# A pre-norm transformer block: four score steps between the last feed-forward products, and a group's evacuation on VectorE

## What is computed

```python
x = x + 0.5 * ffn(layernorm(x))       # 8 experts, each 128 -> 256 -> 128
x = x + attn(layernorm(x))
x = x + 0.5 * ffn(layernorm(x))

# ffn: every token goes through all experts; g = top-1 gate
h = gelu(einsum('nd,edh->neh', xf, w1) + b1)
y = einsum('neh,ehd->ned', h, w2) + b2
out = (y * (g / (g + 1e-6))[:, None, None]).sum(axis=1)

# attn: second layernorm, then
q, k, v = split(xn @ w_qkv);  q, k = l2norm(q), l2norm(k)
o = softmax(causal(8.0 * q @ k.T)) @ v;   return o @ w_out
```

## Time and profile before

| | |
|---|---|
| median of 3 runs | 308.84 us (308.37 to 308.96) |
| the profiled execution | 308.51 us, its span 306.8 us |
| PE busy | 283.4 us (92%) |
| ACT busy | 226.5 us (74%) |
| DVE busy | 218.2 us (71%) |
| POOL busy | 86.4 us (28%) |

### The profile page before, as it was taken

The page is one execution under the profiler, slowest core; times in us unless marked ns, Lnnn a source line. Parts: engine busy times, 40 slices in busy tenths (PEclk is TensorE's granted clock), DMA queues, the critical chain, the costliest instruction groups (busy, mean ns, idle before and its releaser), DMA issues.

```text
span 306.8 us, 5263 instructions
## 1 busy us (share of the span) xinstructions
PE 283.4 (92%) x1699; PEld 198.4 (65%) x1699; DVE 218.2 (71%) x572; ACT 226.5 (74%) x347; POOL 86.4 (28%) x151
## 2 busy tenths in 40 slices
PE   7799999999949997689997989999999999999994
PEld 7588788688738885424432433248888878878882
DVE  5888888979867777695466362118778887888675
ACT  2477777776674776998797889986667787686672
POOL 7243103201860183190406604030230310320010
PEclk9699999999998999979999999999999999999999
DMA  5800000000000000000000000000000100100101
GB/s 166 241 24 3 0 1 2 0 1 0 2 1 0 0 4 0 0 2 0 2 2 1 3 0 2 0 2 0 0 2 1 35 2 0 34 0 0 35 2 34
DMA packets 8044, 4.66 MB, mean 15 GB/s; under 512 B 626, under 2 KB 8020, under 8 KB 8020
## 3 DMA queue, kind: packets, MB, share of 16 engines
q1 hardware_dynamic: 8020, 4.35, 4.9%
HBM read 3.30 MB, written 1.05 MB: 14 GB/s over the span
## 4 chain that ended last, share of the span: by engine, by line
PE 62%; DVE 12%; issue 11%; POOL 8%; ACT 6%; DVEq 0%; POOLq 0%; ACTq 0%
PE ps L412 8%; PE ps L422 8%; PE ps L414 7%; PE ps L413 7%; PE ps L553 7%; PE ps L424 7%; PE ps L423 7%; ACT probs L737 2%; PE ps L532 2%; DVE xn L833 2%; POOL rstd L1122 2%; DVE h_lo L887 2%; PE ps L400 2%; PE ps L590 1%; PE ps L584 1%
## 5 line engine op out<-in xcount | busy, mean ns | idle before, releaser
L724 ACT ACTIVATE h<-ps,cols 128x512 f32<-128x512 f32 x128 | 87.9, 689 | 51.3 <-PE ps L414 45.7
L887 DVE TENSOR_TENSOR h_lo<-h,h_hi 128x512 fp32r<-128x512 f32 x128 | 88.8, 697 | 30.7 <-ACT h_hi L727 27.8
L737 ACT ACTIVATE probs<-ps 128x1024 f32<-128x1024 f32 (+1 forms) x80 | 68.6, 964 | 7.5 <-PE ps L532 7.3
L422 PE MATMUL ps<-h_hi,w_hi 128*128 128x512 f32 x128 | 54.1, 422 | 4.2 <-DVE h_lo L887 3.4
L412 PE MATMUL ps<-xT_hi,w_hi 128*128 128x512 f32 (+1 forms) x128 | 51.9, 406 | 1.4 <-DVE xT_lo L1074 1.4
L414 PE MATMUL ps<-xT_hi,w_lo 128*128 128x512 f32 (+1 forms) x128 | 51.2, 400 | 0.0
L413 PE MATMUL ps<-xT_lo,w_hi 128*128 128x512 f32 (+1 forms) x128 | 51.0, 399 | 0.0
L424 PE MATMUL ps<-h_hi,w_lo 128*128 128x512 f32 x128 | 50.4, 394 | 0.0
L423 PE MATMUL ps<-h_lo,w_hi 128*128 128x512 f32 x128 | 50.4, 394 | 0.0
L727 ACT ACTIVATE h_hi<-ps,cols 128x512 fp32r<-128x512 f32 x72 | 49.1, 681 | 0.0
L1196 POOL TENSOR_SCALAR_AFFINE_SELECT probs<-probs 128x256 f32<-128x256 f32 x64 | 26.3, 434 | 55.2 <-ACT probs L737 54.4
(11 more groups left out here) (127 smaller groups left out, 299.9 us busy)
## 6 DMA issues: line engine op xcount, KB each, us to landing
w_raw<-in_L_ffn_w SPq DMA_DIRECT2D x8, 256.0 KB, 4.3
x_sb<-in_L_attn_x SPq DMA_DIRECT2D x4, 256.0 KB, 6.3
out_x<-x_sb SPq DMA_DIRECT2D x3, 256.0 KB, 2.3
out_x<-x_sb SPq DMA_DIRECT2D x2, 128.0 KB, 1.8
wqkv_sb<-in_L_attn_w_qkv SPq DMA_DIRECT2D x1, 96.0 KB, 4.9
wout_sb<-in_L_attn_w_out SPq DMA_DIRECT2D x1, 32.0 KB, 4.0
small<-in_L_ffn_b SPq DMA_DIRECT2D x1, 8.0 KB
small<-in_L_attn_ln_w SPq DMA_DIRECT2D x1, 0.5 KB
```

What stands on the lines that cost most here:

```text
L422: pe.matmul(y, w2_hi[:, w], h_hi[:, c % RING, :], start=(c == 0), stop=False)
L724: first = nc.scalar.activation(h[:, slot, :], ps[:, BANK_H + slot, :], ACT.Gelu, bias=bias)
L737: nc.scalar.activation(probs[:, s % P_SLOTS, :, 0:width], ps[:, bank:bank + 2, 0:width], ACT.Exp, scale=SCALE).then_inc(exp_done, 1)
L887: dve.tensor_tensor(h_lo[:, slot, :], h[:, slot, :], h_hi[:, slot, :].bitcast(f32), ALU.subtract).then_inc(split_done, 1)
```

## The change

Four things are done at the turn from the last feed-forward group of layer 0 to attention.

- The scores of steps 1, 2 and 3 move forward on PE: step 1 behind the qkv products at chunk 13, step 2 behind down(14), step 3 behind down(15). They, and step 0, use two sets of banks by turns (0 and 1, 2 and 3), so step 2 waits for the exp of step 0, and step 3 for that of step 1. From step 4 on three sets are used in turn again, beginning with banks 4 and 5; `score_set` and `set_reader` say which set and whose exp.
- The exp of step 1 moves in front of `evacuate_y` on ACT.
- The squares and copies of group 2 (six instructions) leave ACT. DVE makes the copies, then the squares from the copy in one instruction of 512 columns.
- In the last group the k copy of group 1 moves from ACT (chunk 12) to DVE (chunk 15).

```diff
--- before.py
+++ after.py
@@ -244,6 +244,14 @@
         jobs += [(quad_steps, "rows", u), (quad_steps, "features", u), (quad_steps, "project", u)]
         assert len({at for at, *_ in jobs}) == len(jobs) - 2
         job_number = {(kind, arg): n for n, (_, kind, arg) in enumerate(jobs)}
+
+        def score_set(s):
+
+            return s % 2 if s < 4 else (s - 2) % S_SETS
+
+        def set_reader(s):
+
+            return s - 2 if s in (2, 3) else None if s == 4 or s < 2 else s - S_SETS
 
         def output_bank(u):
             return 7 - u % 2
@@ -485,6 +493,10 @@
                         ln_transpose(ATT, g - 1, min(g + 2, GROUPS))
                     if operands and g >= 1 and c == at["att_qkv"]:
                         qkv_products(g - 1)
+                    if operands and last and c >= at["att_qkv"]:
+                        if c == at["att_qkv"]:
+                            pe.wait_ge(gelu_done, CHUNKS * GROUPS)
+                        scores(1 + c - at["att_qkv"])
 
             def qkv_products(p):
                 if p == 0:
@@ -521,15 +533,15 @@
 
             def scores(s):
                 st = steps[s]
-                if s >= S_SETS:
-                    pe.wait_ge(exp_done, s - S_SETS + 1)
+                if set_reader(s) is not None:
+                    pe.wait_ge(exp_done, set_reader(s) + 1)
                 for kt, q0, width, at in st["item"]:
                     k0 = SEQ * st["b"] + P * kt
                     qc = SEQ * st["b"] + GROUP * st["qg"] + q0
                     for hd in range(2):
                         j = 2 * st["pair"] + hd
                         rows = slice(ROW * j, ROW * j + ROW)
-                        m = pe.matmul(ps[:, 2 * (s % S_SETS) + hd, at:at + width], kT[rows, st["quad"], k0:k0 + P],
+                        m = pe.matmul(ps[:, 2 * score_set(s) + hd, at:at + width], kT[rows, st["quad"], k0:k0 + P],
                                       qT[rows, st["quad"], qc:qc + width], start=True, stop=True)
                 m.then_inc(scores_done, 1)
 
@@ -622,15 +634,12 @@
                         else:
                             pe.wait_ge(job_emptied, job_number["k_stack", p] + 1)
                     for s in (2 * k, 2 * k + 1):
-                        if s == 0:
+                        if s < 4:
                             continue
-                        if s < S_SETS:
-                            if s == 1:
-                                pe.wait_ge(gelu_done, CHUNKS * GROUPS)
-                            else:
-                                pe.wait_ge(qkv_copied, LAST)
-                                pe.wait_ge(y_evac, GROUPS)
-                                pe.wait_ge(xf_done[FFN], GROUPS)
+                        if s == 4:
+                            pe.wait_ge(qkv_copied, LAST)
+                            pe.wait_ge(y_evac, GROUPS)
+                            pe.wait_ge(xf_done[FFN], GROUPS)
                         scores(s)
                     if k == 0:
                         y_transposes(LAST, BANK_YT_LAST)
@@ -733,7 +742,7 @@
                 if s >= P_SLOTS:
                     act.wait_ge(pv_done, (s - P_SLOTS) // 2 + 1)
                 width = sum(w for _, _, w, _ in steps[s]["item"])
-                bank = 2 * (s % S_SETS)
+                bank = 2 * score_set(s)
                 nc.scalar.activation(probs[:, s % P_SLOTS, :, 0:width], ps[:, bank:bank + 2, 0:width], ACT.Exp,
                                      scale=SCALE).then_inc(exp_done, 1)
 
@@ -760,8 +769,7 @@
                         nc.scalar.activation(table_use[:, 1:2], ones[:, 0:1], ACT.Exp)
                     if operands and c == CHUNKS - 1 and last:
                         exp_scores(0)
-                        square_qk(g - 1)
-                        copy_qkv(g - 1)
+                        exp_scores(1)
                     if c == CHUNKS - 1:
                         evacuate_y(F)
                     if c + LAG < CHUNKS:
@@ -775,7 +783,7 @@
                             copy_qkv(g - 2)
                         if c == at["qk_high"]:
                             high_stacks(g - 2)
-                        if c == at["k_copy"]:
+                        if c == at["k_copy"] and not last:
                             copy_k(g - 2)
                     if operands and g >= 1 and c == at["att_copy"]:
                         affine_features(g - 1)
@@ -801,7 +809,7 @@
             for c in range(LAG):
                 gelu(0, 0, c)
             ffn_groups(nc.scalar, 0, lambda g: ffn_group(0, g))
-            for s in range(1, len(steps)):
+            for s in range(2, len(steps)):
                 exp_scores(s)
             for c in range(LAG):
                 gelu(1, GROUPS, c)
@@ -917,8 +925,27 @@
                 dve.tensor_scalar(rnorm[:, :, :].bitcast(mybir.dt.int32), seed[:, :, :], -1.0, float(0x5F3759DF),
                                   ALU.mult, ALU.add).then_inc(seed_done, 1)
 
+            def copy_k(p):
+                dve.wait_ge(stack_t, p + 1)
+                dve.tensor_copy(kT[:, :, GROUP * p:GROUP * p + GROUP],
+                                ps[:, BANK_KT, :].bitcast(f16).rearrange("p (a q) -> p a q", a=QUADS)).then_inc(kT_done, 1)
+
+            def copy_qkv(p):
+                dve.wait_ge(qkv_mm, p + 1)
+                dve.wait_ge(qkn_done, 2 * p)
+                halves_qkv = [ps[:, bank, 0:384].rearrange("p (t c) -> p t c", t=2) for bank in qkv_banks(p)]
+                for half, qkv in enumerate(halves_qkv):
+                    dve.tensor_copy(qk_raw[:, 2 * half:2 * half + 2, :], qkv[:, :, 0:2 * INNER])
+                for half, qkv in enumerate(halves_qkv):
+                    last = dve.tensor_copy(v_ones[:, 4 * p + 2 * half:4 * p + 2 * half + 2, :, 0:HEAD_DIM],
+                                           qkv[:, :, 2 * INNER:3 * INNER].rearrange("p t (h d) -> p t h d", h=HEADS))
+                last.then_inc(qkv_copied, 1)
+
             def own_squares(p):
-                dve.wait_ge(job_emptied, job_number["qk", p] + 1)
+                if p == LAST:
+                    dve.wait_ge(job_emptied, job_number["qk", p] + 1)
+                else:
+                    dve.wait_ge(qkv_copied, p + 1)
                 dve.tensor_tensor(sq[:, :, :], qk_raw[:, :, :], qk_raw[:, :, :], ALU.mult).then_inc(sq_done, 2)
 
             def stacks(p):
@@ -984,6 +1011,9 @@
                         if c == at["q_copy"]:
                             copy_q(g - 2)
                     if operands and last and c == CHUNKS - 1:
+                        copy_k(g - 2)
+                        copy_qkv(g - 1)
+                        own_squares(g - 1)
                         square_sums(g - 1)
                         guesses(g - 1)
                     if layer == 1 and first:
```

## The result

| | before | changed |
|---|---|---|
| median, 4 runs each | 308.61 us (308.31 to 308.96) | 310.66 us (310.49 to 310.81) |
| ratio | | 1.0066 (95% interval 1.0048 to 1.0083) |
| profiled execution, span | 308.51, 306.8 | 310.49, 308.8 |

The changed kernel is slower by 0.7%, 2.0 us between the two profiled spans. I had forecast 309.2; 310.66 is inside the range, which ended at 310.8, and outside the forecast's own case (308.9 to 309.4). I had given "slower" 0.33. The forecast difference was 0.4 us, the measured one 2.0.

What follows compares the result with a forecast made beforehand. Attention's early part was taken to hang on the residual of group 3 and DVE's unbroken work to oT. Insertions of about 0.8 less 0.41 gave +0.4, DVE copies and lead 0: median 309.2 us, range 308.2 to 310.8.

Steps and rivals of the forecast that it cites:

- the forecast's own case: At the turn to attention, the summed terms hold: +0.1 to +0.6 us, 308.9 to 309.4; chance 0.48.
- The lead of ACT: Exp 2 on ACT starts 0.7 us earlier, but PE waits for oT at "rows 0": worth 0 in the total.
- DVE's added work: K copy, four qkv copies and squares on DVE, hidden ahead of the residual with 0.2 us to spare: 0.
- the price of an insertion: Scores put between PE's last products cost 0.32 to 0.43 us each, 0.64 to 0.86 for two, delaying down(15).
- the case of a slow clock: PE's longer wait before "rows 0" brings a 1.2 GHz stretch behind it: 1.3 us on top, 310.5; chance 0.22.
- The credit of 0.41 for ACT no longer being the last: Before yT, ACT had been late by 0.41 us; moving its copies away offsets that much of the insertions' cost.
- the term of +0.42: yT on ACT runs 0.42 us later, from 127.25 instead of 126.83, bounds +0.25 to +0.5.
- that rival of my own text: The clock falls behind PE's longer wait at "rows 0": 1.3 us on top, 310.5; chance 0.22.
- DVE did not become the last: Rival at the residual: dearer copies or POOL make it wait for DVE, 0.2 to 0.5 us more, 309.5; chance 0.13.
- The turn did move: Rival at the turn: inserted scores cost PE only some 0.2 us each, yT comes as before, 308.8; chance 0.05.
- The lead was not kept: Rival at "rows 0": where PE comes late, ACT's 0.7 us carries on, down to 308.1; chance 0.12.
- the 0.2 us I had set beside the sum: POOL's mask of step 1 would delay DVE's squares by up to 0.42, giving a total of 309.4, not 309.2.

Runs made afterwards that it cites:

- with products filled in: Changed kernel plus eight discarded 512-column matmuls ahead of "rows 0", in PE's wait for oT: 309.71 us, 1.0017 to the kernel before.
- scores alone: Kernel before with scores of steps 1 to 3 moved ahead and exp 1 before the squares; k copy, squares and copies stay on ACT: 311.30 us, 1.0063.
- scores behind: Changed kernel with scores 1 and 2 behind down(15), step 3 behind the transposes of yT, exp 1 behind yT: 310.06 us, 1.0026 to the kernel before.
- evacuation alone: Kernel before with only the k copy of group 1 and the copies and squares of group 2 moved to DVE: 309.13 us, 1.0000.
- the runs near 91 and 139: Discarded matmuls in PE's waits: sixteen in group 2 of the kernel before (306.87 us, 0.9929); eight ahead of "rows 0" in the changed kernel (309.71 us, 1.0017).
- the base: Kernel before with discarded matmuls in group 2 (sixteen), ahead of scores 4 to 7, "rows 0" (two) and "rows 3" (five): 308.45 us, 0.9974.

## Why the prediction was right and where it was wrong

The measured 310.66 is in the range, but only because the range took in the case of a slow clock, which had 0.22. The forecast's own sum gave +0.4 us. The runs show 0.8 to 0.9 at the turn, and the rest is the clock.

**Right: the path.** The chain went from yT through the residual and DVE's unbroken work to oT. In the earlier trace rows that work takes 9.7 us, and in the changed kernel it takes 9.75 (130.24 to 139.99). The lead of ACT was 0.55 us (exp 2 at qkv + 4.60, against 5.15 before), and it ended at "rows 0", where PE waited 1.44 and 2.25 us in the two profiles of the changed kernel. DVE's added work ended at qkv + 4.94, where I had 5.0, and was hidden.

**Wrong: the price of an insertion.** I took 0.32 to 0.43 each, 0.64 to 0.86 for two, from the one insertion of the earlier trace rows. The two cost 1.05, and the rows of PE show where. From the start of the qkv products to the next instruction it takes 1.47 us where scores follow (124.61 to 126.08), and 1.24 where down(14) does (123.49 to 124.73): 0.23. The scores themselves take 0.32 (126.08 to 126.40), as in the earlier trace rows. Down(14) with the second insertion behind it takes 1.22 (126.40 to 127.62) against 0.83 without (124.73 to 125.56): 0.39. The first to the last product of down(15) takes 0.57 (127.62 to 128.19) against 0.46 (125.56 to 126.02): 0.11. Of the 0.39, 0.32 are again scores (127.30 to 127.62). So the two insertions cost 0.32 each, as I had it at the low end, and the forms next to them 0.41 in all (0.23, 0.07 and 0.11), where I had allowed 0.22 at the high end. The credit of 0.41 for ACT no longer being the last came out at 0.37 (1.05 less the 0.68 of yT). A term I did not have is 0.15: transposes of yT start 0.94 behind yT, not 0.79. That gap is 0.94 to 1.01 us in every profile with step 2 ahead of the transposes (the changed kernel twice, with products filled in, scores alone, scores behind), and 0.74 to 0.79 in those of before and of the evacuation alone. What makes it was not tried. In all the term of +0.42 measured +0.87.

**Wrong: the chance of the clock.** I gave the slow stretch behind the wait 0.22. It shows in the second profile of the changed kernel, in those of the scores alone and of the scores behind down(15), and its removal brings 1.5 us. I had priced it at 1.3. The argument against it, PE's 1.69 us of idle time before the qkv products with the clock at 1.00, was one wait taken as a rule; the wait at "rows 0" came out as 1.44 and 2.25 us, on both sides of it, and only the longer had the slow stretch behind it. The length of the wait is not all that differs between these two: where it was 1.44, a slow stretch had run from 131 to 135 us just before. I had also written that both cases in the trace of before fit the rule of a long wait. They do not: the slow stretch at 132.28 came behind waits of no more than 0.90 us (at 129.72), and the longer wait of 1.69 us had none behind it. What I missed altogether is the slow stretch near 91 us: the prediction does not mention it, and its length moves the rest of the kernel by over 1 us from one execution to another. Of the two profiles of the changed kernel, the one that escaped the long stretch there paid at 139; that every execution pays at one place or the other is more than two profiles show. By that rival of my own text the time would be 310.5, and 310.66 was measured; the fastest of all ten executions of the changed kernel was 310.49. That the two numbers are so close is partly luck: in the first profile none of the 2.0 us is the slow clock behind "rows 0", 0.87 is the turn and 1.12 the longer stretch near 91.

**The other rivals.** DVE did not become the last: the residual was released by the transposes. The turn did move. The lead was not kept, although what I had named for it does happen: in the second profile of before, with a slow stretch from 130 to 137 us, PE did not wait for oT but came 0.56 us after its copy (138.19 to 138.75). In no profile of the changed kernel without discarded products is it so.

**The rule on DVE and POOL.** The mask of step 1 took 0.80 us instead of 0.42, beside the squares:

```profile
127.60 0.80 POOL L1226 TENSOR_SCALAR_AFFINE_SELECT probs<-probs 128x256 f32<-128x256 f32 x1 [1.34 <-ACT probs L746]
```

The squares had started at 127.44 and kept their 0.69. In the run of the scores alone, where DVE makes no squares, the same mask takes 0.41:

```profile
126.26 0.41 POOL L1206 TENSOR_SCALAR_AFFINE_SELECT probs<-probs 128x256 f32<-128x256 f32 x1 [0.49 <-ACT probs L746]
```

It is the Trainium skill's rule ("SBUF — State Buffer", Who interferes with whom) with the sides changed: the one that comes second waits, and here that was POOL, so the 0.2 us I had set beside the sum did not come. The other page of the Trainium skill ("TensorE: Matmul & The Clock Gate", Loop structure matters more than you think) agrees with the runs near 91 and 139: products behind a long wait ran cold (granted clock 0.66 over 138 to 143), and filling the wait kept the clock (1.00). It does not tell which of this kernel's short waits have such products behind them.

## What to carry to other kernels

Before moving work of PE ahead of a product, see what waits for that product: here two short scores were put in front of the one that started 9.7 us of serial work on DVE, to feed an engine whose lead ended at the next wait. An idle stretch of PE has a second price, the slow products behind it; filling the two waits in group 2 with products that nobody reads gained 0.7%, more than any reordering tried. And when times of one kernel spread by more than the effect looked for, compare profiles from a common instruction on. The mean clock sorts the times of one kernel here, but between two kernels it says little: what a slow stretch costs depends on whether PE is the last where it falls.

## What the runs showed of the hardware

- The same instructions at the same times (91.3 us in both kernels) ran into slow stretches that ended at 94.7 or at 97.1, with 1.12 us between the two outcomes. Both kernels had short and long ones in their two profiles each, so the order of the instructions does not decide which.
- A wait of PE of 1.44 us ahead of "rows 0" left the clock at 2.4 GHz, where a slow stretch had ended just before; waits of 1.90, 2.21 and 2.25, with no slow stretch just before, were followed by 1.2 GHz. With the wait cut to 0.20 by discarded products it stayed at 2.4.
- The length of a wait alone does not decide it: PE's wait of 1.33 or 1.34 us ahead of "rows 2" is in all fourteen profiles, and four of them have a slow stretch of 3.4 us behind it, ten have none.
- Discarded products cost time where PE is or becomes the last: in the base, with ten of them ahead of the scores of steps 4 to 7 and two ahead of "rows 0", PE went from waiting 0.6 us for oT to starting 0.8 after its copy.
